# A reordered prologue: four combined weight products side by side in four PSUM banks, operands in quarters, and the fourth batch moved into steps 5 to 15

## The reference

```python
h = layernorm(x) * (1 + ca) + sa                       # sa, ca, ga, ...: silu(c) @ wmod
q = h @ Wq.T                                           # 32 heads of 128
c_kv = h @ Wdk.T                                       # then k_c = c_kv @ Wupk.T, v = c_kv @ Wupv.T
k = rope channels from h @ Wkr.T, the others from k_c  # 8 key heads
attn = softmax(causal(q @ k.T / sqrt(128)))
x = x + ga * ((attn @ v) @ Wo.T)
h = layernorm(x) * (1 + cb) + sb
logits = h @ router.T + bias;  s = softmax(logits);  top 8 of 64
x = x + gb * (h * sum(top8) + top8_weights @ expert_bias)
```

## Time and profile before

| | |
|---|---|
| median of 3 runs | 1459.76 us (1459.34 to 1461.4) |
| the profiled execution | 1460.17 us, its span (first to last instruction) 1458.9 us |
| busy over the span | PE 98%, DVE 79%, POOL 70%, ACT 69% |
| first matmul | 9.54 us after the span's start |

### The profile page before, as it was taken

One profiled execution on the slowest core, in us unless ns is written; L12 is line 12 of the kernel. 1 busy time (PEld: TensorE's weight loads), 2 busy tenths in 40 slices (PEclk: granted clock), 3 DMA queues, 4 the chain that ended last, 5 costly groups with the idle time before them and its releaser, 6 DMA issues.

```text
span 1458.9 us, 24651 instructions
## 1 busy us (share of the span) xinstructions
PE 1431.4 (98%) x7150; PEld 1208.2 (83%) x7150; DVE 1154.3 (79%) x3544; ACT 1007.9 (69%) x2389; POOL 1023.6 (70%) x805
## 2 busy tenths in 40 slices
PE   7989999999999999999999999999999999999998
PEld 7877888888888888888888888888888888888876
DVE  5697777787777777777777777777779989888876
ACT  5667666766676676777676677676667677776673
POOL 3768766776676677677676677676588888886662
PEclk9999999999999999999999999999999999999999
DMA  9478766775677767676587668658878989899881
GB/s 308 162 210 248 219 203 182 238 230 167 198 224 206 198 213 229 195 212 201 177 234 217 216 180 225 193 170 263 236 232 264 268 285 285 262 265 268 267 234 48
DMA packets 215157, 322.03 MB, mean 221 GB/s; under 512 B 42512, under 2 KB 132464, under 8 KB 215024
## 3 DMA queue, kind: packets, MB, share of 16 engines
q1 hardware_dynamic: 214736, 320.39, 73.2%
q10 hardware_dynamic: 288, 0.07, 0.0%
HBM read 179.43 MB, written 140.95 MB: 220 GB/s over the span
## 4 chain that ended last, share of the span: by engine, by line
PE 88%; DVE 4%; POOL 2%; DMA 2%; issue 2%; ACT 2%; SPq 1%; DVEq 0%; ACTq 0%
PE bank_s L633 22%; PE bank_o L793 22%; PE bank_pv L743 14%; PE bank_s L699 13%; PE bank_s L665 5%; PE bank_s L650 5%; PE bank_s L695 1%; POOL PT_lo L1835 1%; PE bank_s L606 1%; PE bank_s L849 1%; DVE y L1539 1%; DVE blocks L1487 0%; PE bank_s L696 0%; DMA wc_scratch<-wc_out 0%; PE bank_o L606 0%
## 5 line engine op out<-in xcount | busy, mean ns | idle before, releaser
L1835 POOL TENSOR_TENSOR PT_lo<-PT_raw,PT_hi 128x640 fp32r<-128x640 f32 x246 | 382.4, 1577 | 30.1 <-ACT PT_hi L1125 30.1
L1111 ACT ACTIVATE probs<-probs,row_inv 128x512 f32<-128x512 f32 (+3 forms) x512 | 257.8, 553 | 193.9 <-DVE row_inv L1470 193.7
L1823 POOL TENSOR_TENSOR rot_c<-rot_c,rot_s 128x512 f32<-128x512 f32 x128 | 167.3, 1307 | 256.8 <-DVE rot_s L1427 256.8
L1104 ACT ACTIVATE probs<-probs,row_min 128x384 f32<-128x384 f32 (+3 forms) x512 | 281.6, 552 | 48.6 <-DVE row_min L1463 48.5
L1487 DVE STREAM_TRANSPOSE blocks<-probs 128x384 f32<-128x384 f32 x508 | 213.8, 446 | 19.7 <-ACT probs L1111 14.1
L699 PE MATMUL bank_s<-kT_both,qT_hi 128*128 128x512 f32 (+2 forms) x768 | 215.2, 341 | 2.7 <-DVE row_min L1463 1.0
L1463 DVE CUSTOM_DVE_ANT_0 probs<-bank_s,mask 128x512 f32<-128x512 f32 (+2 forms) x384 | 205.4, 552 | 0.8 <-issue 0.3
L1828 POOL TENSOR_TENSOR qT_lo<-rot_c,qT_hi 128x512 fp32r<-128x512 f32 x128 | 166.8, 1304 | 50.8 <-ACT qT_hi L1086 49.9
L793 PE MATMUL bank_o<-wo_lo,OT_hi 128*128 128x512 f32 x496 | 195.7, 394 | 2.2 <-DMA wo_lo<-split_wo 1.7
L633 PE MATMUL bank_s<-hT_lo,wq_hi 128*128 128x512 f32 x484 | 194.8, 403 | 2.2 <-DVE row_min L1463 1.4
L793 PE MATMUL bank_o<-wo_hi,OT_hi 128*128 128x512 f32 x496 | 194.1, 391 | 0.0
(11 more groups left out here) (315 smaller groups left out, 3255.8 us busy)
## 6 DMA issues: line engine op xcount, KB each, us to landing
blocks<-blocks SPq DMA_DIRECT2D x127, 640.0 KB, 3.4
PT_raw<-blocks SPq DMA_DIRECT2D x500, 160.0 KB, 3.9
stage<-in_wq SPq DMA_DIRECT2D x32, 256.0 KB, 5.1
vblocks<-kv_raw SPq DMA_DIRECT2D x32, 256.0 KB, 5.4
kv_raw<-vblocks SPq DMA_DIRECT2D x128, 64.0 KB, 2.2
stage<-in_wo SPq DMA_DIRECT2D x32, 256.0 KB, 5.1
split_wq<-wq_hi SPq DMA_DIRECT2D x32, 256.0 KB, 5.2
split_wq<-wq_lo SPq DMA_DIRECT2D x32, 256.0 KB, 5.5
```

Of the source, the lines that this page charges most:

```text
L1104: ins = act.activation(row(t, qt), row(t, qt), ACT.Exp, bias=row_min[m][:, qt:qt + 1], scale=-1.0, accum_out=row_sum[m][:, qt:qt + 1])
L1111: ins = act.activation(row(t, qt), row(t, qt), ACT.Copy, scale=row_inv[t % 2][:, qt:qt + 1])
L1823: pool.tensor_tensor(rot_c[:], rot_c[:], rot_s[:], ALU.add).then_inc(pool_a, 1)
L1835: pool.tensor_tensor(lo[:, at], raw_of(t)[:, at], hi[:, at].bitcast(F32), ALU.subtract).then_inc(pool_t, 1)
```

## The change

- Start: `combine_first` makes products 0 to 3 together, chunk by chunk, in the banks s3, s2, o2 and o3, the hi x hi pass first. `wup_in[0]` is now loaded, copied and subtracted in four quarters of 384 columns, in turn with the quarters of `wdk` (`split_both`, `load_up0`, `load_down`). The small DVE work on `c_exp` and three memsets come after these. The semaphores of `wup` are counted anew, and the quarters share theirs with the later rows (`d_up0_rows`).
- The fourth batch: loading, statistics, normalising, transposing, modulating and splitting leave the prologue. The load is issued in step 4, DVE's statistics are in steps 5 to 8, POOL's in step 9, ACT's normalising in steps 10 and 11, the transposes and DVE's modulation in steps 12 to 15 (bank s1), the splits one step later.
- New orders up to step 4 on all five queues; the hand-written part now ends with step 5, so that `step` starts at t = 6 on PE and t = 5 on ACT, DVE and POOL. `scores(6)` stands before `values_pair(1, UPPER)` and `values_pair(1, LOWER)` directly behind it. `store_combined(15)` stands behind the loads of `PT_raw` for heads 0 and 1. The stores of the first split weights move from steps 1, 2, 4 to 4, 6, 8.

The diff, cut to its core:

```diff
-COMBINE_BANKS = ["s3", "s2"] * (SOON // 2) + ["o0", "o1"] * ((COMBINED - SOON) // 2)
+COMBINE_BANKS = (["s3", "s2", "o2", "o3"] + ["s3", "s2"] * ((SOON - CH) // 2)
+                 + ["o0", "o1"] * ((COMBINED - SOON) // 2))
...
-LATE_SPLITS = 6
+LATE_STATS = 5
+LATE_NORMAL = LATE_STATS + QT + 1
+LATE_TRANSPOSES = LATE_NORMAL + 2
...
+            def combine_first():
+                for m in range(CH):
+                    for k in (2, 0, 1):
+                        if k == 2:
+                            pe.wait_ge(split_w, 2 * m + 2)
+                        else:
+                            pe.wait_ge(split_lo, 2 * m + 2)
+                        for c in range(CH):
+                            down, up = passes(wdk, (wup_hi[0], wup_lo[0]))[k]
+                            mm = pe.matmul(bank[COMBINE_BANKS[c]][:, 0:2 * KVC], down[:, m, c * P:(c + 1) * P], up[:, m, :],
+                                           start=(m == 0 and k == 2), stop=(m == CH - 1 and k == 1))
...
+                pe.wait_ge(act_comb, i - 3 if i < CH + 2 else i - 1)
...
+            combine_first()
+            combine(4)
+            combine(5)
             modulation(0)
+            transpose_h(0)
+            combine(6)
             modulation(1)
...
+            out_pair(0, UPPER, [2])
             out_pair(0, UPPER, [3])
             q_proj(7)
             out_pair(0, LOWER)
+            scores(6, tile_order(6))
             values_pair(1, UPPER)
-            for t in range(5, BY_PE):
+            values_pair(1, LOWER)
+            q_proj(8)
+            k_proj(2)
+            out_pair(1, UPPER)
+            for t in range(6, BY_PE):
                 step(t)
...
+            def split_both(m):
+                act.wait_ge(d_up0_rows[m], UP0)
+                act.activation(wup_hi[0][:, m, :], wup_in[0][:, m, :], ACT.Copy).then_inc(split_w, 1)
+                act.wait_ge(d_wdk[m], 16)
+                act.activation(wdk[0][:, m, :], wdk_in[:, m, :], ACT.Copy).then_inc(split_w, 1)
...
             sp.wait_ge(pe_comb, COMBINED)
             load_transposed(0)
             load_transposed(1)
+            store_combined(15)
             for s in d_wc:
                 sp.wait_ge(s, 16 * (COMBINED // 4))
...
+                if t == LATE_STATS - 1:
+                    load_x(SHARED)
```

More of the change, by code:

```diff
@@ L468, in build @@
         d_modT = sem("d_modT")
-        d_rows = [sem(f"d_rows{b}") for b in range(BATCH)]
+        d_up0_rows = [sem(f"d_up0_rows{b}") for b in range(BATCH)]
+        UP0 = 16
         d_out = [sem(f"d_out{i}") for i in range(F_RING)]
@@ L895, in step @@
                     out_pair(t // 2 - 1, UPPER)
+                if late_chunk(t) is not None:
+                    pe.wait_ge(dve_s, score_read(t + 1, 0))
+                    transpose_h(late_chunk(t))
                 if t in MOD_STEPS:
@@ L940, in tensor_program @@
             q_proj(0)
+            transpose_h(6)
+            pe.wait_ge(pool_h, CH)
+            k_proj(0)
             transpose_h(7)
@@ L1313, in scalar_program @@
             split_moved_hi(1)
-            normalise(2, 0)
-            normalise(2, 1)
-            q_split(4)
-            k_split(1)
             exponentials(3, 0)
             exponentials(3, 1)
-            pair_split_hi(0, UPPER)
-            for g, i in pieces(2):
-                split_chunk(g, i)
+            split_chunk(0, 0)
+            split_h(11)
             normalise(3, 0)
             normalise(3, 1)
-            for t in range(3, BY_PE):
+            split_chunk(0, 1)
+            pair_split_hi(0, UPPER)
+            q_split(5)
+            exponentials(4, 0)
+            exponentials(4, 1)
+            normalise(4, 0)
+            normalise(4, 1)
+            split_moved_hi(2)
+            q_split(6)
+            split_chunk(0, 2)
+            split_moved_hi(3)
+            pair_split_hi(0, LOWER)
+            exponentials(5, 0)
+            exponentials(5, 1)
+            split_chunk(0, 3)
+            normalise(5, 0)
+            normalise(5, 1)
+            for t in range(5, BY_PE):
                 step(t)
@@ L2031, in store_modulation, with load_up0, load_down, load_first_modulation @@
                     store_row(GATED_SCALE_ROW, mod_row)
+            def load_up0(m):
+                sp.dma_start(wup_in[0][:, m, :], A["wup"][0][:, m, :]).then_inc(d_up0_rows[m], UP0)
+            def load_down(m):
+                sp.dma_start(wdk_in[:, m, :], A["wdk"].rearrange("(c p) n -> p c n", p=P)[:, m, :]).then_inc(d_wdk[m], 16)
+            def load_first_modulation(c):
+                sp.dma_start(wmod[0][:, c, :], wmod_v[MOD_PIECES[0]][:, c, :]).then_inc(d_wmod0[c], 16)
             def load_wup(n):
@@ L2240, in sync_program @@
                         store_split(g, i)
[L2242 removed]
+                for i in {4: [4, 5], 6: [6, 7], 8: [8, 9]}.get(t, []):
                     store_split(-1, i)
```

340 lines of the change are left out of this document (189 added, 151 removed).

## The result

| | before | after |
|---|---|---|
| median of 4 runs | 1460.36 us (1459.34 to 1461.4) | 1468.79 us (1466.77 to 1470.73) |
| ratio, 95% interval | | 1.0053 (1.0041 to 1.0065) |
| profiled execution, its span | 1460.17, 1458.9 us | 1468.44, 1467.1 us |
| first matmul | 9.54 us | 5.36 us |
| first score matmul of step 6 (the landmark) | 129.85 us | 131.85 us |

What follows compares the result with a forecast made beforehand. TensorE, busy 98% of the span, was taken as the bound: its start, work and waits. Start -4.0, early orders +2.5 and turn +4.6 gave +3.1 us, so 1462.8 us, range 1457.2 to 1466.2.

Steps and rivals of the forecast that it cites:

- Start: First matmul: TensorE starts at 5.5 us, 4.0 us earlier than before.
- The slow phase: First matmuls at the 1.2 GHz clock: slow for 3.6 us as before; bound 1.9 us lost if slow until 13.2 us.
- Early orders: Before the loop, TensorE meets its suppliers: waits of 2.9 us against 0.3 before, +2.5 us (0.5 to 4).
- the walk: TensorE followed to the first score matmul of step 6: 131.4 us, against 129.85 before; chance 0.52 within 1.5 us.
- The turn: From values_pair(0, UPPER) to values_pair(1, LOWER): five waits of 3.0, 1.3, 4.4, 0.9 and 1.5 us, 11.1 against 6.5, +4.6.
- the sign of a wait over 4 us there: At out_pair(0, LOWER): a PE wait of over 4 us on OT_lo would show the forecast right.
- the fourth batch: Transposes 12 to 15, behind the landmark: 1.5 us of work, nothing for the other engines' part, 1 us as bound.
- Rival (a): At the turn: no worse than today, waits of 6.5 us, 1458.2 or 1455.7 us; chance 0.14 in full, below 1456.8.
- my 1463.2: Whole kernel: forecast time of the profiled execution, span 1462.0 us with the 1.3 us around it.
- The 0.4 us taken off for the median: Whole kernel: the profiled execution lies 0.4 us above the median, so 1463.2 becomes 1462.8 us.
- My chance of 0.46 for slower: Whole kernel: chance 0.46 that it measures slower, beside 0.40 for the same and 0.14 for faster.

Runs made afterwards that it cites:

- the second trace of the changed kernel: The changed kernel measured once more, with nothing altered; 1469.8 us, ratio 1.0057.
- e5: Changed kernel with TensorE's first matmul held until all eight subtractions of the quarters are through; 1472.4 us, ratio 1.0082.
- e4: Changed kernel with the fourth batch's POOL statistics ahead of q_rope in step 9 and ACT's normalising in idle stretches of steps 10 and 11; 1466.1 us, 1.0029.
- e9: Changed kernel with the third wo chunk behind everything TensorE waits for, on both ACT and POOL; 1466.5 us, ratio 1.0037.
- e10: Changed kernel with e9, e8 and e4 together and the fourth quarter of wmod issued ahead of store_combined(0); 1461.3 us, ratio 1.0002.
- e2: Kernel before with the late fourth batch alone, in steps 4 to 15, start and orders as before; 1466.9 us, ratio 1.0037.
- e1: Kernel before with the quartered start alone, both modulations directly behind it; 1462.4 us, ratio 1.0004.
- e3: Changed kernel with ACT's split of the first LOWER pair ahead of the third wo chunk and head 3's PT_hi; 1470.1 us, ratio 1.0053.
- e6: Changed kernel with ACT's first LOWER split and head 5's exponentials ahead of the third wo chunk and head 3's PT_hi; 1470.0 us, 1.0059.
- e7: e6 with scores(6) between the two parts of values pair 1; 1468.8 us, ratio 1.0050.
- e8: Changed kernel with store_combined(15) between the loads of PT_raw for heads 0 and 1; 1466.9 us, ratio 1.0037.
- e12: e10 with the fourth batch's whole part four steps later, its load in step 8; 1472.1 us, ratio 1.0071.
- e13: e10 with the fourth batch's load in four transfers of 256 KB, in steps 4 to 7; 1461.6 us, ratio 1.0004.

## Why the prediction was right or wrong

**Start**: right. 4.2 us earlier for 4.0; ACT's first two copies ran from 4.26 to 5.30 us.

**The slow phase**: it lasted from 5.36 to 10.6 us, where 3.6 us were taken from the earlier trace rows. That costs 5.3 - 3.6 us at half pace, 0.8 us, inside the bound of 1.9. In the second trace of the changed kernel it was 3.2 us long and in e5 2.8 us. The Trainium skill, "TensorE: Matmul & The Clock Gate", Part 1, has it that its length differs between runs of one kernel; these traces agree.

**Early orders**: size right, reason wrong in part. The waits were 0.7, 0.6, 0.8 and 0.9 us for the 0.3, 0.9, 0.5 and 0.9 taken. Each costs more than the view of waits shows, by an estimate 0.16 us: a matmul of 512 columns takes 0.39 us in the rows and the next starts 0.23 us after it, but behind a wait the two don't overlap; the walk left that out. And only the one for `wmod` comes from starting early (e5). With the slow phase this makes the last combined product end at 78.5 us instead of 76.4. For `q_proj(0)`, the POOL split at 29.62 us met a DVE subtraction at 29.51: two splits took 4.04 us, where two took 2.54 us elsewhere, and the wait was 0.78 us. That lies between the 0.5 taken and the 1.1 by the rule of the Trainium skill, "SBUF — State Buffer", section Who interferes with whom; the long POOL operation agrees with the rule.

**The turn**: right in three of its five waits, with luck in the landmark. 2.8 us for 3.0 at `values_pair(0, UPPER)`, 1.6 for 1.3, 2.6 for 4.4 at `out_pair(0, LOWER)` and nothing for 0.9 at `scores(6)`, 1.5 for 1.5. TensorE came to `values_pair(0, UPPER)` 1.7 us later than forecast, out of the early stretch, and the waits of the turn are 2.6 us shorter than the 11.1 forecast: 8.5 us. The 1.8 us that the third wait was short came back as slow matmuls behind it (1.6 us), a term that the walk did not have. That the landmark is right to 0.5 us is these misses cancelling; the walk's own terms, added up again, give 131.7 us and not 131.4. OT_lo of the LOWER pair came at 112.10 us for 112.4 forecast, but the sign of a wait over 4 us there did not come.

**The step that failed is the fourth batch**: "I take nothing for it, 1 us as the bound". The reason given was that DVE, ACT and POOL had idle time enough. The lag grew by 4.9 us from head 7 to head 20 where 1.5 were taken for the transposes alone. The transposes are 1.8 (0.42 to 0.50 us each by the lag). Five waits are 0.4 (DVE's statistics), 0.6 (POOL's statistics), 1.0 (ACT's normalising), 0.5 and 0.4 (DVE's modulation), 2.9 together. Each costs 0.05 to 0.2 us beyond its idle time, 0.6 in all, and 0.5 go off again at heads 10 and 20, where the kernel before is the slower one. e4 takes the second and the third wait away with nothing but places; these two had cost 2.0 us. An engine's idle share says nothing of who stands behind the added instruction in its queue; here it was each time the operand for which TensorE came next. I had priced ACT's part as a bound, and POOL's and DVE's not at all.

**What the walk had not priced either** is the load. In the changed kernel it costs TensorE nothing: it is issued at 117.93 us, the eight loads of `PT_raw` not before 123.88, ACT waits 0.5 us for each head and TensorE for neither. It costs as soon as TensorE is earlier and the loads follow in 2 to 3 us: the lag grows at head 8 by 2.2 us in e9, 3.0 in e10 and 3.6 in e2, 0.4 of each being DVE's statistics.

**Rival (a)**, that the turn would be no worse, fell. **The rest**: of the 5.2 us by which the profiled execution missed my 1463.2, 0.5 are at the landmark, 3.4 in steps 7 to 20, and 1.3 behind head 20. Of these, two steps of 0.35 us, by head 44 and by head 92, are in both traces of the changed kernel and in neither before nor e1: there `q_proj` waits 0.31 us for DVE's `row_min` (518.01 and 1021.04 us). Another 0.6 come behind head 127, where the wait for the load of `wo_lo` is 2.3 us for 1.7 before (1.9 in the second trace). Why DVE is late at the two heads stays open. The 0.4 us taken off for the median came from three executions; with the fourth the profiled one lies 0.2 us below it. My chance of 0.46 for slower was on the right side, but the range ended 2.6 us short of the measurement.

## What to carry to other kernels

Work moved into a saturated loop is priced by what stands directly behind it in each queue that it enters, not by how idle the engines are; the same instructions cost 2.0 us less when they stood a few places earlier. When a wait goes away, look for the same transfer in the queue of the next engine before you count the gain: here one weight chunk held ACT and, two runs later, POOL. A start that comes earlier is worth what the order behind it can use: nothing with one order (e1), 3.3 of 5.6 us with another (e5).

## What the runs showed of the hardware

The granted clock of TensorE fell to its lower level (1.2 GHz) in the middle of the kernel behind some pauses of 1.7 us and more, and not behind others of the same length:

| the pause stands ahead of | it fell behind | it did not fall behind |
|---|---|---|
| `values_pair(0, UPPER)` | 2.0 us (e3), 2.8 (changed, second trace), 3.2 (e6), 3.2 (e9) | 2.8 (changed), 2.9 (e7), 3.0 (e5), 3.1 (e4), 1.5 to 1.7 (e8, e10, e12, e13) |
| `out_pair(0, LOWER)` | 2.6 (changed), 2.6 (e4), 2.7 (e8), 3.1 (e5), 3.3 (changed, second trace) | |
| `scores(6)` or `values_pair(1, UPPER)` | 3.8 (e3), 3.8 (e6), 3.7 (e7) | 1.8 (before), 1.8 (e1), 1.9 (e2) |
| the last output product, near 1425 us | 1.7 (before) and 1.7 to 2.5 in ten other traces | 1.7 (e10), 2.0 (e2), 2.0 (e9), 2.1 (e13) |
| elsewhere | 2.3 (e1, 20 us), 2.1 and 5.5 (e12, 179 and 291 us) | 2.0 (e2, 138 us) |

From `values_pair(0, UPPER)` to the first matmul of `scores(5)` it is 7.86 to 7.88 us in the four traces with the fall and 6.28 or 6.29 in the five without it: 1.6 us. Behind `out_pair(0, LOWER)` a fall cost 1.3 to 1.6 us, and the longest, behind the 3.8 us of e6, 2.4. So a pause of 2 us cost up to 1.8 times its length (2.0 and 1.6 in e3), and two executions of one program differed by such a fall.

A transfer of 1 MB issued 2 to 3 us ahead of eight small ones held them so that ACT waited 3.3 us (e10) and 3.9 us (e2); issued 6 us ahead of them (changed) it left 0.5, and with only a quarter of it in front (e13) the wait was 0.8. The Trainium skill, "DMA: Bandwidth & Descriptors", section Two DMAs through the same engine are not ordered, says that descriptors of one queue of a DMA engine start in order, and all of these are issued by SP. The traces agree so far as the later transfers were the ones held; the descriptors themselves no view shows.
